# Expert weights per slot tile, gates at the slots and adding gathers in a decoder block

## The reference

```python
gates = softmax(xf @ router_w)
top_v, top_i = top_k(gates, 2)
masked = zeros_like(gates).at[arange(N)[:, None], top_i].set(top_v)
masked = masked / (masked.sum(-1, keepdims=True) + EPS)
# _ffn: silu((x * rsqrt(mean(x*x) + eps) * rms_w) @ W1) @ W2
routed_out = einsum('end,ne->nd', vmap(_ffn)(rms_w, w1, w2), masked)
return routed_out + shared
```

## Time and profile before

| | |
|---|---|
| Median of 3 runs | 1147.33 us (1137.47 to 1151.03) |
| The profiled execution | 1151.23 us |
| Its span, first to last instruction | 1149.5 us |
| Granted TensorE clock, mean of the span | 0.897 |
| PE / DVE / ACT / POOL busy | 84% / 67% / 50% / 38% |
| HBM read and written | 78.40 MB, 22.41 MB |

### The profile page before, as it was taken

How to read it: one execution, slowest core, us unless ns; L and a number is a source line. 1 busy time by engine, 2 the same in 40 slices (tenths; PEclk the granted TensorE clock), 3 DMA queues, 4 the chain that set the end, 5 groups by cost and what they waited for, 6 DMA issues and landing times.

```text
span 1149.5 us, 17879 instructions
## 1 busy us (share of the span) xinstructions
PE 964.5 (84%) x5249; PEld 797.5 (69%) x5249; DVE 768.8 (67%) x1970; ACT 580.1 (50%) x1359; POOL 438.3 (38%) x536
## 2 busy tenths in 40 slices
PE   7899999999985998772776178886969999999994
PEld 7899999999963555551554067886656888888883
DVE  2566666666658524431567599962767989988984
ACT  2566666666655423231567144423644555555554
POOL 3365656656564124434526076761460000000002
PEclk9999999999997799996687579896777999999997
DMA  7122323223232002221100243600105665666640
GB/s 218 62 97 97 103 75 103 98 84 109 81 117 85 28 20 57 62 56 42 37 10 1 63 101 75 59 1 1 55 1 156 165 180 160 180 169 175 176 137 36
DMA packets 52833, 101.42 MB, mean 88 GB/s; under 512 B 7201, under 2 KB 27873, under 8 KB 52274
## 3 DMA queue, kind: packets, MB, share of 16 engines
q1 hardware_dynamic: 50322, 95.79, 29.5%
q0 software_dynamic: 2464, 5.05, 1.9%
HBM read 78.40 MB, written 22.41 MB: 88 GB/s over the span
## 4 chain that ended last, share of the span: by engine, by line
PE 40%; POOL 19%; issue 18%; DVE 14%; ACT 4%; DMA 3%; SPq 1%; POOLq 0%; DVEq 0%; ACTq 0%
PE PS L1628 8%; PE PS L1629 8%; PE PS L1630 8%; POOL P L610 7%; POOL WS L619 3%; PE PS L1840 3%; PE PS L1824 3%; POOL WS L615 2%; DMA Wb<-decay 2%; DVE r0b L1443 2%; DVE rb L1456 2%; POOL rs L411 1%; PE PS L1772 1%; PE PS L1778 1%; ACT Xp L418 1%
## 5 line engine op out<-in xcount | busy, mean ns | idle before, releaser
L610 POOL TENSOR_TENSOR P<-P,rl 128x256 f32<-128x256 f32 (+1 forms) x130 | 104.8, 827 | 126.6 <-DVE rl L1112 126.6
L408 POOL TENSOR_SCALAR ms<-mv 128x4 f32<-128x4 f32 x24 | 5.6, 231 | 336.1 <-DVE mv L401 325.9
L1031 ACT ACTIVATE FG<-PS 128x512 f32<-128x512 f32 x120 | 72.0, 600 | 111.0 <-PE PS L1630 111.0
L1105 DVE CUSTOM_DVE_ANT_0 P<-PS,cmask 128x128 f32<-128x128 f32 (+1 forms) x260 | 77.1, 352 | 70.8 <-issue 70.8
L828 ACT ACTIVATE P<-P,mn 128x128 f32<-128x128 f32 (+1 forms) x260 | 114.3, 443 | 2.4 <-DVE mn L1105 2.4
L1628 PE MATMUL PS<-XTh,W 128*128 128x512 f32 x256 | 101.7, 397 | 0.4
L1629 PE MATMUL PS<-XTl,W 128*128 128x512 f32 x256 | 101.1, 395 | 0.0
L1630 PE MATMUL PS<-XTh,W 128*128 128x512 f32 x256 | 101.0, 395 | 0.0
L1698 PE MATMUL PS<-VO,PT 128*128 128x128 f32 x804 | 100.6, 275 | 0.0
L1614 DVE TENSOR_TENSOR FU<-FG,PS 128x512 f32<-128x512 f32 x120 | 82.6, 688 | 25.2 <-PE PS L1630 25.2
L1698 PEld LDWEIGHTS PS<-VO,PT 128*128 128x128 f32 x804 | 95.0, 192 | 0.0
(11 more groups left out here) (423 smaller groups left out, 2658.5 us busy)
## 6 DMA issues: line engine op xcount, KB each, us to landing
GI<-coef SPq DMA_DIRECT2D x60, 256.0 KB, 4.1
GW<-coef SPq DMA_DIRECT2D x60, 256.0 KB, 4.1
w3s<-WS SPq DMA_DIRECT2D x32, 384.0 KB, 2.6
W<-w3s SPq DMA_DIRECT2D x32, 384.0 KB, 3.2
Wb<-decay SPq DMA_DIRECT2D x8, 1024.0 KB, 14.9
WR<-in_w SPq DMA_DIRECT2D x32, 192.0 KB, 2.5
WR<-in_w SPq DMA_DIRECT2D x16, 256.0 KB, 2.8
w12f<-WS SPq DMA_DIRECT2D x16, 256.0 KB, 2.1
```

The lines of the kernel that those rows point to most:

```text
L610: last = pool.tensor_tensor(v, v, f, ALU.mult)
L1031: act.activation(FG[:, k % 2, :], bank(4 + k % 2), ACT.Silu).then_inc(sem("fg_done"), 1)
L1105: dve.tensor_tensor_reduce(out=P[:, slot, c:c + w], in0=scores(par, q), in1=cmask[:, 256 - w:256], scale=1.0, scalar=3e38, op0=ALU.add, op ...
```

## The change

- The routed experts' weights are no longer resident. SyncE reads the expert of each slot tile into a register and loads its 256 KB into a ring of four (`WT`); the slot of the ring is free when the tile four before has its down product. PE no longer reads registers. The two shared experts stay resident (`WS0`, 512 KB).
- In a step of the slot loop PE makes the up product ahead of the transpose of the gathered tile.
- The gates are computed ahead of the loop, carried to the slots by 32 further one-hot products (`SLOT_GATE`), and ACT scales `Y` by them. The Exp moves among the Silus of the shared experts; ranks and one-hot products stand at earlier steps.
- The gathers back add into `X` in the DMA (`compute_op=add`), for each chunk first all of the first experts, then, when these have landed, the second. `combine` is gone; its statistics (`combined_stats`) stand a tile earlier, the scaling, transposes and second roundings of the next chunk too. Two of the eight softplus sums stand at t = 14.
- The decay weights of batch 0 come from `weights_out` and two copies on ACT instead of DRAM.

```diff
+        WS0 = sb("WSh", [128, E0 - E0R, 2 * HID], F32, sc)
+        WT = [sb(f"WT{r}", [128, 2 * HID], F32, sc) for r in range(RING)]
...
-        GATES_EXP = 6
-        RANKS_AT, HOT_AT = 2, (7, 8, 9, 10)
+        GATES_EXP = 9
+        RANKS_AT, HOT_AT = 0, (5, 6, 8, 9)
...
+            def expert_in(j):
+                e = sp.value_load(tei[0:1, j:j + 1], min_val=0, max_val=E0R - 1)
+                if j >= RING:
+                    sp.wait_ge(sem("yt_ready"), on("yt_ready", j - RING + 1))
+                sp.dma_start(WT[j % RING][:, :], w12f[ds(e + (E0 - E0R), 1), :, :].rearrange("o p n -> p (o n)")).then_inc(sem(f"wt_in{j % RING}"), 16)
+
+            sp.wait_ge(sem("te_done"), on("te_done", 1))
+            for j in range(RING - 1):
+                expert_in(j)
             for j in range(NT):
+                if j + RING - 1 < NT:
+                    expert_in(j + RING - 1)
...
-            for g in range(B):
+            for g in range(1, B):
...
-            def rows_back(t):
-                for s in range(2):
-                    pool.indirect_dma_start(out=YG[:, s, t, :], out_offset=None, in_=yrows,
-                                            in_offset=bass.IndirectOffsetOnAxis(ap=pidx[:, s, t:t + 1], axis=0)).then_inc(sem(f"yg_in{t // 4}"), 16)
+            def rows_back(s, c):
+                for t in tiles(c):
+                    pool.indirect_dma_start(out=X[:, t, :], out_offset=None, in_=yrows, compute_op=ALU.add,
+                                            in_offset=bass.IndirectOffsetOnAxis(ap=pidx[:, s, t:t + 1], axis=0)).then_inc(sem(f"y{'ab'[s]}_in{c}"), 16)
 
             pool.wait_ge(sem("pidx_done"), on("pidx_done", 1))
+            pool.wait_ge(sem("shared_added"), on("shared_added", NC_))
             for r in range(RING):
                 pool.wait_ge(sem(f"ys_out{r}"), on(f"ys_out{r}", (NT - r + RING - 1) // RING * 16))
-            for t in range(T):
-                rows_back(t)
-                if t in (5, 9, 13, 15):
-                    ln_factors(pool, 2, (t - 4) // 4 if t < 15 else 3)
+            for c in range(NC_):
+                rows_back(0, c)
+                if c:
+                    ln_factors(pool, 2, c - 1)
+                pool.wait_ge(sem(f"ya_in{c}"), on(f"ya_in{c}", 64))
+                rows_back(1, c)
+            ln_factors(pool, 2, NC_ - 1)
...
-                act.activation(Y[j % RING][:, :], slot_y, ACT.Copy).then_inc(sem("yt_done"), 1)
+                act.activation(Y[j % RING][:, :], slot_y, ACT.Copy, scale=gslot[:, j:j + 1]).then_inc(sem("yt_done"), 1)
...
+            for h in range(2):
+                act.wait_ge(sem("w_bc"), h + 1)
+                act.activation(half(Wb[0], h), FW, ACT.Copy).then_inc(sem("w0_out"), 1)
...
+            for n in range(2):
+                gates_step(n)
+            dve.wait_ge(sem("tok_ready"), 1)
+            dve.tensor_copy(tok[:, :], SLOT_TOK).then_inc(sem("tok_done"), 1)
+            dve.tensor_copy(pidx[:, :, :], pslot[:, :, :]).then_inc(sem("pidx_done"), 1)
+            for n in range(2, 16):
+                gates_step(n)
+            after_last()
+            for s in range(2):
+                dve.tensor_tensor(eqJ[:, s, :, :], eqJ[:, s, :, :], bt(gAB[:, s, :], NT), ALU.mult).then_inc(sem("gated_hot"), 1)
+            dve.wait_ge(sem("gates_ready"), 1)
+            dve.tensor_copy(gslot[:, :], SLOT_GATE).then_inc(sem("gslot_done"), 1)
...
-            def combine(c):
-                dve.wait_ge(sem(f"yg_in{c}"), 128)
-                dve.wait_ge(sem("shared_added"), on("shared_added", NC_))
-                after_last()
-                for s in range(2):
-                    for t in tiles(c):
-                        if s:
-                            dve.wait_ge(sem("combined"), on("combined", 8 * c + t % 4 + 1))
-                        dve.scalar_tensor_tensor(X[:, t, :], YG[:, s, t, :], gAB[:, s, t:t + 1], X[:, t, :],
-                                                 ALU.mult, ALU.add).then_inc(sem("combined"), 1)
-                dve.wait_ge(sem("combined"), on("combined", 8 * c + 8))
+
+            def combined_stats(c):
+                dve.wait_ge(sem(f"yb_in{c}"), 64)
                 ln_stats(dve, 2, c)
...
+            combined_stats(0)
             ln_lo(dve, 2, 0)
             for t in range(T):
                 p = t % 2
+                if t % 4 == 0 and t < T - 4:
+                    combined_stats(t // 4 + 1)
                 dve.wait_ge(sem("qs_done"), t + 1)
                 dve.wait_ge(sem("dk_ready"), t + 1)
                 dve.tensor_tensor(PR[:, p, :], bank(2 + p), QS[:, p, :], ALU.mult).then_inc(sem("pr_done"), 1)
...
                 dve.tensor_scalar(ZR[:, t, :], bank(6 + p), 0.0, None, ALU.max).then_inc(sem("z_pos"), 1)
                 dve.wait_ge(sem("pr_done"), t + 1)
                 dve.tensor_reduce(ABs[:, 1, t, :], PR[:, p, :].rearrange("p (h d) -> p h d", h=H1), AX.X, ALU.add).then_inc(sem("b_sum"), 1)
-                if t % 4 == 1 and t < T - 4:
-                    combine(t // 4 + 1)
+                if t % 4 == 2 and t < T - 4:
+                    ln_lo(dve, 2, t // 4 + 1)
                 if t % 4 == 3:
-                    if t < T - 4:
-                        ln_lo(dve, 2, t // 4 + 1)
                     signed_values(t // 4)
-            for t in range(0, T, 2):
+                if t == T - 2:
+                    softplus_sums(0, 2)
+                    softplus_sums(2, 4)
+            for t in range(4, T, 2):
...
-            def expert_of(j):
-                return pe.value_load(tei[0:1, j:j + 1], min_val=E0 - E0R, max_val=E0 - 1)
-
             def slot_up(j):
-                e = expert_of(j)
+                pe.wait_ge(sem(f"wt_in{j % RING}"), on(f"wt_in{j % RING}", j // RING * 16 + 16))
                 pe.wait_ge(sem("xt_done"), on("xt_done", j + 1))
                 if j:
                     pe.wait_ge(sem("hs_done"), on("hs_done", j))
-                pe.matmul(slot_h, xTs[j % 2][:, :], WE[:, ds(e, 1), 0:HID].rearrange("p o n -> p (o n)"),
-                          start=True, stop=True).then_inc(sem("hs_ready"), 1)
+                pe.matmul(slot_h, xTs[j % 2][:, :], WT[j % RING][:, 0:HID], start=True, stop=True).then_inc(sem("hs_ready"), 1)
...
+            for s in range(2):
+                pe.wait_ge(sem("gated_hot"), on("gated_hot", s + 1))
+                for t in range(T):
+                    last = pe.matmul(SLOT_GATE, eqP[:, s, t, :], eqJ[:, s, t, :], start=s == 0 and t == 0,
+                                     stop=s == 1 and t == T - 1, skip_group_check=True)
+            last.then_inc(sem("gates_ready"), 1)
+            pe.wait_ge(sem("gslot_done"), on("gslot_done", 1))
             for i in range(NT + 3):
+                if 1 <= i < NT + 1:
+                    slot_up(i - 1)
...
+                if t % 4 == 2 and t < T - 4:
+                    if t > 4:
+                        pe.wait_ge(sem("vp_done"), t // 4 * 2)
+                    ln_transpose(pe, 2, t // 4 + 1)
...
+            def weights_out(g, h, first=False):
+                if first:
+                    if h:
+                        pe.wait_ge(sem("w0_out"), on("w0_out", 1))
+                elif 2 * g + h >= 1:
                     pe.wait_ge(sem("scan2_done"), 2 * g + h)
+                else:
+                    pe.wait_ge(sem("w0_out"), on("w0_out", 2))
...
+            for h in range(2):
+                weights_out(0, h, first=True)
```

More of the change, by code:

```diff
@@ L88, in decoder_program @@
         "shared_added": ("bo_added", 4),
-        "combined": ("q_elu", 8),
+        "ya_in0": ("xg_in0", (NT + 3) // RING * 16),
+        "ya_in1": ("xg_in1", (NT + 2) // RING * 16),
+        "ya_in2": ("xg_in2", (NT + 1) // RING * 16),
+        "ya_in3": ("xg_in3", NT // RING * 16),
+        "gslot_done": ("q_done", 4),
+        "gated_hot": ("xl_done", B + 1 + 4),
+        "w0_out": ("z_exp", T),
+        "wt_in0": ("xT_in", 16),
+        "wt_in1": ("x_in", 16),
+        "wt_in2": ("rw_in", 16),
+        "wt_in3": ("wr_in", 16),
         "rank_ready": ("consts", 8),
@@ L219, in decoder_program @@
         eqJ = sb("eqJ", [128, 2, T, NT], F32, sx)
+        idJ = sb("idJ", [128, 2, T, NT], F32, sx)
+        gslot = sb("gslot", [128, NT], F32, sx)
         cmpJ = sb("cmpJ", [128, NT, E0R], F32, sx)
@@ L339, in decoder_program @@
         NEG = -3e38
-        SLOT_TOK = bank(7)[:, 256:256 + NT]
+        SLOT_TOK, SLOT_GATE = bank(7)[:, 256:256 + NT], bank(7)[:, 384:384 + NT]
         RANK, TOTAL = bank(6)[:, 0:E0R * T], bank(6)[:, 256:256 + E0R * T]
@@ L877, in _ @@
                 act.activation(Hf[:, n % 4, :], bank(4 + n % 2), ACT.Silu).then_inc(sem("sg_done"), 1)
+                if n == GATES_EXP:
+                    act.wait_ge(sem("lg_sub"), 1)
+                    act.activation(Lg[:, :, :], Lg[:, :, :], ACT.Exp).then_inc(sem("lg_exp"), 1)
+            act.wait_ge(sem("gslot_done"), on("gslot_done", 1))
             def slot_silu(j):
@@ L894, in _ @@
```

(34 more changed lines are left out.)

19 lines of the change are left out of this document (3 added, 16 removed).

## The result

The changed kernel takes 1203.85 us (median of 4 runs, 1200.24 to 1205.68), the kernel before 1148.38 (4 runs): a ratio of 1.050, 95% interval 1.043 to 1.057. The forecast was 1177 with a range to 1200. The profiled run took 1200.24, its span is 1198.5 (49.0 longer than before), its mean clock 0.856 instead of 0.897. The medians lie 55.5 apart: the profiled run is the fastest of its four, and the one before was above its median.

A forecast was written before the change was run, and what follows sets the result against it. Named limits: register-read waits in the slot loop, second-layer projections with no engine full, and waits for decay weights. Terms 56.2 + 1.6 - 18.8 - 9.4 = +29.6 on the median 1147.33 gave 1177 us, range 1144 to 1200.

The forecast's parts named there:

- The slot loop: Routed experts' loop: 41 steps ruled by the weight ring at 3.41 us each; last store 56.2 us later.
- P = (L + S) / (k - 2): Slot loop: mean step P, PE's own step S, ring depth k; forecast for four slots as (L + 1.73) / 2.
- L: Slot loop: time from a down product's end to the landed weights, forecast at 4.30 us.
- the middle between 3.02 and 3.80: Slot loop: mean step at full and at lower clock; the clock was expected to swing, so 3.41 us.
- Ahead of the loop: Before the slot loop: 32 more one-hot products and a copy start it 8.1 us later, at 431.7.
- Behind the loop: Last store to first projection product: twelve gathers at the plain price plus one landing wait, +1.6 us.
- My upper bound of +6.6: Behind the slot loop: a landing of 4.1 us instead of 1.6, twice in a row.
- Rival E: Adding gathers slow, 1.25 becoming 2.5: 15 us more before the first factors, most of the 18.8 lost; 1205, chance 0.08.
- The projections: Second layer's projections: without combine and with earlier statistics, 63.8 us instead of 82.6, so -18.8.
- POOL just keeps up: Second layer's projections: POOL's eight gathers and factors take 12 us per chunk.
- Decay: First scan: batch 0's weights from PE and ACT, then batch 1's load landing in 13.5 us; -9.4 us.

The follow-up runs named there:

- e2: The changed kernel with gathers as plain copies over X, the addition left out of the computation; 1175.6 us, beside 1150.0 for the kernel before.
- e4: The kernel before with only batch 0's decay weights taken from PE and ACT; 1139.1 us, beside 1150.0 for the kernel before.
- e11: The changed kernel, ring of four, with plain gathers and the additions done on DVE; 1179.3 us, beside 1146.1 for the kernel before.
- e12: The changed kernel with a ring of six, plain gathers added on DVE, and SyncE's load ahead of the store; 1108.5 us, beside 1146.1 before.
- e1: The changed kernel with a ring of six weight buffers in place of four, nothing else; 1138.5 us, beside 1150.0 for the kernel before.
- e7: The changed kernel with a ring of six and plain gathers added on DVE; 1118.2 us, ratio 0.975 to the kernel before.
- e9: The changed kernel, ring of four, with SyncE issuing the load ahead of the store; 1152.4 us, beside 1146.1 for the kernel before.
- e6: The changed kernel with a ring of five weight buffers in place of four; 1154.7 us, beside 1147.2 for the kernel before.
- e13: The changed kernel with one useless PE product of 256 columns behind each down product from step 12; 1189.2 us, beside 1146.1 before.

## Why the prediction was wrong

The direction was right, and so was the mechanism of the slot loop. The size was not: 1177 forecast, 1204 measured, outside the range. By its own steps:

- **The slot loop: the right mechanism, the number partly by luck.** Forecast +56.2 for the last store, measured +55.1. The form P = (L + S) / (k - 2) held for depths of three, four and five. Of L the parts were: copy of Y 0.38 (I had 0.28 and 0.06 of handing over), SyncE from store to load 1.09 (1.16), landing 2.6 to 2.8 (2.8), together 4.14 (4.30). The mean step was 3.41 as forecast, but not for the forecast's reason. I took the middle between 3.02 and 3.80, as if the clock were low half of the time. The clock was 0.56 to 0.64 from 470 on, so low for most of it, and a step at the low clock is 2.73, not 3.30: behind the up product I doubled 1.04 to 2.08, where the ring of three has 1.50 (three transposes of 0.21 and a down product of 0.87). (4.14 + 2.73) / 2 is 3.44. Two errors cancelled.
- **Ahead of the loop: close, by luck.** +7.3 for +8.1, but 2.8 of it is this run's faster start; the edit itself costs 10.3. The forecast took the price of the one-hot products at the full clock, and they ran at a falling one.
- **Behind the loop: the step that failed.** "An add has no row; I take the price of a plain gather." An add has another price in POOL's time, 1.84 instead of 1.24. Twelve gathers stand ahead of the first factors: 12 x 0.60 = 7.2, and 1.6 + 7.2 = 8.8 is what was measured. My upper bound of +6.6 widened the landing alone, and the landing was not the trouble: the one wait for it was the 1.6 forecast. Rival E named the slow add, with 0.08.
- **The projections: the same term again.** "POOL just keeps up" rested on the plain price. The real period is 16.8 a chunk; between the first and the third factors 16 gathers x 0.60 = 9.6 of the 11.5 us are missing by that. With plain gathers and the same wait between the passes (e2) it is 24.3 to the first product and 64.5 from there, where the forecast has 22.6 + 1.6 = 24.2 and 63.8. So in this stretch only the add's price was wrong.
- **Decay: small.** -7.5 for -9.4: batch 1's load took 15.87 (15.24 in e4), I gave it 13.5.

With the add at its measured price the forecast's sum is 29.6 + 7.2 + 9.6 = 46.4, beside the 49.0 between the profiled runs; 1.9 each in the projections and the decay weights make up most of the rest. What went wrong in the odds: rival E priced the add at "1.25 becoming 2.5" and got 0.08, though no row spoke against it. That its 1205 is so near the measured time is luck: the add cost 0.60 more, not 1.25. An operation that the trace doesn't show, 32 times on a queue that "just keeps up", deserved much more, and the range should have reached its case.

## What to carry to other kernels

Count a ring's depth from the event that frees a slot to the event that needs it, in steps of the pipeline: here two of four slots were gone, and two more took 62 us off the loop. On a queue that starts loads, put what a later step waits for ahead of what nobody waits for soon (35 us off the loop for the exchange of load and store with four slots, 8 with six). And before moving arithmetic into a DMA, price its issue on the engine that issues it: DVE did in 0.69 us for four tiles what cost 0.60 us of POOL for each.

## What the runs showed of the hardware

- An indirect gather of 128 rows of 512 bytes that adds takes POOL 1.54 us, a plain one 0.94, and lands in 3.3 instead of 2.5 (medians of the changed kernel, of e2 and e11). The Trainium skill, "DMA: Bandwidth & Descriptors", section "SDMA does more than copy", describes the addition as done by a unit inline with the data. No run here shows that unit; what the runs show is the issue on POOL, and it was the larger part. The DMA view, of 584 to 660 us in the changed kernel and of 575 to 660 in e2, shows another difference: for the same 2.10 MB in 32 gathers (packets, MB, share of the engines) the adding ones are 4.5 times as many packets. Whether this is what holds POOL longer is not shown.

```profile
q0 software_dynamic: 4608, 2.10, 23.0%
...
q0 software_dynamic: 1024, 2.10, 9.4%
```

- Reading the register on SyncE took 0.51 from 438.19 to 438.70, where PE's waits had been 0.61 each. The Trainium skill, "DMA: Bandwidth & Descriptors", section "Latency and other measured facts", has a floor of some 600 ns; the 0.51 measured is below it.
- The copy from PSUM with a scale per partition takes 0.37, without it 0.28.
- The landing of 256 KB grows with the traffic, by the medians: 2.6 (ring of three, 56 GB/s), 2.7 (four, 117), 3.1 (five, 165), 3.5 (e12, 192). It is not the traffic alone: with the same loop and ring of six e1 has 3.9 at 178 GB/s and e7 3.3 at 175.
- A store on SyncE takes 0.33 in the changed kernel and 0.43 in e9 and e12, where it follows a load directly (medians; the longest is 1.98, in e9). That order is not all of it: e7, with loads and stores in the changed kernel's order, has 0.43 too, and e6 one store of 1.78.
- 64 records of one-hot products (128x45, f32) that kept PE busy for 6.70 of 7 us ran at a mean clock of 0.61; a loop with pauses ran at 0.56, and at 0.94 once the pauses were partly filled (e13).
